# Projections of q, k and v as three float32r products of split operands

## The reference

```
xn  = (x - mean) / sqrt(var + 1e-5)                 # over the 256 features
kqv = xn @ Wqkv + bqkv                              # 256 -> 768
q, k, v = kqv as (b, s, 3, 16 heads, 16)
scores = einsum('bsnh,btnh->bnst', k, q) / 4
scores = triu(scores) - 10000 * tril(ones, -1)
attn = softmax(scores, axis=2)
out  = einsum('bnkq,bknh->bqnh', attn, v) @ Wo + bo
ffn  = fp8(xn / in_scale) * in_scale @ (w8 * w8_scale).T
result = x + out + ffn
```

## Time and profile before

| | |
|---|---|
| time, median of 3 runs | 254.98 us (254.64 to 255.24) |
| span of the profiled execution | 251.8 us; its time around the span is not listed apart |
| TensorE busy (products) | 188.6 us, 75% |
| VectorE busy | 181.1 us, 72% |
| GpSimd busy | 101.3 us, 40% |
| ScalarE busy | 96.5 us, 38% |
| mean granted TensorE clock | 0.897 of 2.4 GHz |
| chain of waits, by engine | TensorE 41%, VectorE 20%, SyncE's queue 16%, issue 8%, DMA 8%, GpSimd 4%, ScalarE 2% |

### The profile page before, as it was taken

One profiled execution on the slowest core, in us unless ns is written; L12 is line 12 of the kernel. 1 busy time (PEld: TensorE's weight loads), 2 busy tenths in 40 slices (PEclk: granted clock), 3 DMA queues, 4 the chain that ended last, 5 costly groups with the idle time before them and its releaser, 6 DMA issues.

```text
span 251.8 us, 5223 instructions
## 1 busy us (share of the span) xinstructions
PE 188.6 (75%) x1725; PEld 140.4 (56%) x1725; DVE 181.1 (72%) x371; ACT 96.5 (38%) x167; POOL 101.3 (40%) x127
## 2 busy tenths in 40 slices
PE   5685026103949898899699969996999698789893
PEld 5564024003736576578477847783878375555572
DVE  3999108501999797987979797978497958995342
ACT  3242200000434464355345623752356135435530
POOL 6605000000488429524842564274425642622410
PEclk9799557555699999999999999997799889999999
DMA  5941696084024734661546273346052725001002
GB/s 187 281 140 38 182 270 167 20 189 110 2 85 120 189 87 127 148 179 46 164 107 171 76 204 95 116 124 178 18 161 80 198 51 157 4 0 46 3 3 83
DMA packets 30102, 28.99 MB, mean 115 GB/s; under 512 B 3008, under 2 KB 26500, under 8 KB 30084
## 3 DMA queue, kind: packets, MB, share of 16 engines
q1 hardware_dynamic: 30084, 28.75, 42.2%
HBM read 17.11 MB, written 10.75 MB: 111 GB/s over the span
## 4 chain that ended last, share of the span: by engine, by line
PE 41%; DVE 20%; SPq 16%; issue 8%; DMA 8%; POOL 4%; ACT 2%; DVEq 1%; POOLq 0%; ACTq 0%
SPq L322 10%; PE pso L984 6%; DVE row_max L732 6%; DMA k_stack<-k_scratch 5%; PE bankA L1072 4%; PE bankA L1009 4%; PE bankB L1009 4%; PE ps L960 3%; PE ps L937 3%; SPq L379 3%; SPq L368 3%; DMA q_scratch<-q_parts 3%; PE ps L939 2%; PE ps L965 2%; DVE neg_parts L750 2%
## 5 line engine op out<-in xcount | busy, mean ns | idle before, releaser
L479 POOL TENSOR_SCALAR_AFFINE_SELECT probs<-probs 128x512 f32<-128x512 f32 (+1 forms) x48 | 38.0, 792 | 122.4 <-ACT probs L541 122.4
L732 DVE TENSOR_REDUCE row_max<-ps 128x4 f32<-128x1024 f32 (+1 forms) x48 | 58.2, 1216 | 28.3 <-PE ps L932 25.1
L541 ACT ACTIVATE probs<-ps 128x1024 f32<-128x1024 f32 x48 | 49.0, 1024 | 72.0 <-PE ps L960 67.7
L932 PE MATMUL ps<-k_stack,q_stack 125*128 125x128 bf16 x128 | 10.6, 230 | 33.1 <-DMA k_stack<-k_scratch 29.9
L932 PEld LDWEIGHTS ps<-k_stack,q_stack 125*128 125x128 bf16 x128 | 8.8, 102 | 35.1 <-issue 30.6
L937 PE MATMUL ps<-k_stack,q_stack 96*128 96x128 bf16 x128 | 20.3, 236 | 5.1 <-DVE row_max L732 5.1
L984 PE MATMUL pso<-probs,v_sb 128*32 128x256 f32 x256 | 21.8, 414 | 0.1
L960 PE MATMUL ps<-q_stack,k_stack 99*128 99x256 bf16 x128 | 20.8, 290 | 0.5 <-issue 0.5
L939 PE MATMUL ps<-k_stack,q_stack 125*128 125x128 bf16 x128 | 20.2, 234 | 0.0
L1009 PE MATMUL bankB<-xT,wqk_sb 128*128 128x256 f32 x64 | 17.7, 423 | 1.4 <-ACT xT L589 1.4
L937 PEld LDWEIGHTS ps<-k_stack,q_stack 96*128 96x128 bf16 x128 | 13.2, 106 | 8.6 <-DVE row_max L732 8.1
(11 more groups left out here) (129 smaller groups left out, 387.8 us busy)
## 6 DMA issues: line engine op xcount, KB each, us to landing
k_stack<-k_scratch SPq DMA_DIRECT2D x32, 192.0 KB, 4.0
q_scratch<-q_parts SPq DMA_DIRECT2D x32, 128.0 KB, 2.0
k_scratch<-k_parts SPq DMA_DIRECT2D x32, 128.0 KB, 1.9
q_stack<-q_scratch SPq DMA_DIRECT2D x16, 256.0 KB, 4.0
q_stack<-q_scratch SPq DMA_DIRECT2D x16, 192.0 KB, 3.0
out_dram<-y SPq DMA_DIRECT2D x8, 256.0 KB, 3.0
x_all<-in_L_attn_x_dram SPq DMA_DIRECT2D x1, 1536.0 KB, 9.0
x_all<-in_L_attn_x_dram SPq DMA_DIRECT2D x2, 256.0 KB, 3.1
```

The lines of the kernel that those rows point to most:

```text
L479: pool.affine_select(out=v, in_=v, compare_op=ALU.is_ge, fill=0.0, base=0, pattern=[[0, heads], [1, P]], channel_multiplier=-1).then_inc(c ...
L541: act.activation(probs[:, i % 2, :], ps[:], ACT.Exp, scale=SCALE).then_inc(exp_done, 1)
L732: dve.tensor_reduce(dst, src, AX_X, ALU.max).then_inc(max_done, 1)
L932: mm = pe.matmul(ps[:, h * P:h * P + P], q_stack[0:K_MAX, par, hh, 0:P], k_stack[0:K_MAX, par, hh, 0:P], start=True, stop=True)
```

## The change

Each of xT and the weights gets a high part, rounded to float32r by a copy, and a low part, the difference. A projection is then low weights by high x, high weights by low x, and high by high, all in float32r, added up in PSUM: 12 matmuls where there were 4 float32 products. The low part of x is made by VectorE, which waits for ScalarE's second copy (xT itself, which `clip_x` still reads), so that the two engines don't read bank B together.

```diff
@@ ScalarE, xT_out @@
+                act.activation(xT_hi[:, par], bank["B"][:].rearrange("p (k s) -> p k s", k=KT), ACT.Copy).then_inc(xT_hi_ready, 1)
                 act.activation(xT[:, par], bank["B"][:].rearrange("p (k s) -> p k s", k=KT), ACT.Copy).then_inc(xT_ready, 1)
@@ ScalarE, startup @@
-                ins = act.activation(wqk_sb[:, k].rearrange("p (m d h) -> p m d h", m=2 * KT, d=HD),
+                ins = act.activation(wqk_hi[:, k].rearrange("p (m d h) -> p m d h", m=2 * KT, d=HD),
...
+            act.wait_ge(wv_landed, 2 * 16)
+            act.activation(wv_hi[:], wqkv_sb[:, :, 2 * D:], ACT.Copy).then_inc(wv_hi_ready, 1)
@@ VectorE @@
+            def xT_low(b, par):
+
+                dve.wait_ge(xT_ready, b + 1)
+                wait(dve, v_mm, b - 1)
+                dve.tensor_tensor(xT_lo[:, par], bank["B"][:].rearrange("p (k s) -> p k s", k=KT),
+                                  xT_hi[:, par].bitcast(F32), ALU.subtract).then_inc(xT_lo_ready, 1)
+
+            def weights_low():
+
+                dve.wait_ge(w_ordered, 1)
+                for k in range(KT):
+                    ins = dve.tensor_tensor(wqk_lo[:, k].rearrange("p (m d h) -> p m d h", m=2 * KT, d=HD),
+                                            wqkv_sb[:, k, 0:2 * D].rearrange("p (m h d) -> p m d h", m=2 * KT, d=HD),
+                                            wqk_hi[:, k].bitcast(F32).rearrange("p (m d h) -> p m d h", m=2 * KT, d=HD), ALU.subtract)
+                ins.then_inc(wqk_lo_ready, 1)
@@ VectorE, run: behind negate_and_split(n, 1), ahead of maxima(n + 1, 1) @@
+                if st.does("xT"):
+                    xT_low(n + 2, p)
@@ VectorE, startup @@
+                    weights_low()
+                    xT_low(0, 0)
...
             rest1(0, 0, "k", "A")
+            xT_low(1, 1)
...
             rest1(1, 1, "k", "A")
+            dve.wait_ge(wv_hi_ready, 1)
+            dve.tensor_tensor(wv_lo[:], wqkv_sb[:, :, 2 * D:], wv_hi[:].bitcast(F32), ALU.subtract).then_inc(wv_lo_ready, 1)
@@ TensorE, project_qk @@
-                pe.wait_ge(xT_ready, b + 1)
+                pe.wait_ge(xT_hi_ready, b + 1)
+                pe.wait_ge(xT_lo_ready, b + 1)
...
                     for k in range(KT):
-                        mm = pe.matmul(dst[:, m * S:m * S + S], wqk_sb[:, k, col:col + P], xT[:, par, k, :],
-                                       start=(k == 0), stop=(k == KT - 1))
+                        pe.matmul(dst[:, m * S:m * S + S], wqk_lo[:, k, col:col + P], xT_hi[:, par, k, :],
+                                  start=(k == 0), stop=False)
+                        pe.matmul(dst[:, m * S:m * S + S], wqk_hi[:, k, col:col + P], xT_lo[:, par, k, :],
+                                  start=False, stop=False)
+                    for k in range(KT):
+                        mm = pe.matmul(dst[:, m * S:m * S + S], wqk_hi[:, k, col:col + P], xT_hi[:, par, k, :],
+                                       start=False, stop=(k == KT - 1))
```

More of the change, by code:

```diff
@@ L33 @@
 F32 = mybir.dt.float32
+F32R = mybir.dt.float32r
 I32 = mybir.dt.int32
@@ L169, in build @@
         wqkv_sb = sb("wqkv_sb", [P, KT, 3 * D])
-        wqk_sb = sb("wqk_sb", [P, KT, 2 * D])
+        wqk_hi = sb("wqk_hi", [P, KT, 2 * D], F32R)
+        wqk_lo = sb("wqk_lo", [P, KT, 2 * D], F32R)
+        wv_hi = sb("wv_hi", [P, KT, D], F32R)
+        wv_lo = sb("wv_lo", [P, KT, D], F32R)
         wo_sb = sb("wo_sb", [P, KT, D])
@@ L207, in build @@
         xT = sb("xT", [P, 2, KT, S])
+        xT_hi = sb("xT_hi", [P, 2, KT, S], F32R)
+        xT_lo = sb("xT_lo", [P, 2, KT, S], F32R)
         x_over = sb("x_over", [P, KT, S])
@@ L266, in build @@
         xn_ready, xT_mm, xT_ready = sem("xn_ready"), sem("xT_mm"), sem("xT_ready")
+        xT_hi_ready, xT_lo_ready = sem("xT_hi_ready"), sem("xT_lo_ready")
+        wqk_lo_ready, wv_hi_ready, wv_lo_ready = sem("wqk_lo_ready"), sem("wv_hi_ready"), sem("wv_lo_ready")
         q_mm, k_mm, v_mm = sem("q_mm"), sem("k_mm"), sem("v_mm")
@@ L284, in build @@
         out_landed = [sem(f"out_landed{p}") for p in range(2)]
-        read = {"xT": (xT_ready, 1, 1), "q": (rest_ready, 2, 1), "k": (rest_ready, 2, 2),
+        read = {"xT": (xT_lo_ready, 1, 1), "q": (rest_ready, 2, 1), "k": (rest_ready, 2, 2),
                 "v": (v_ready, 1, 1), "max_h0": (max_rows_ready, 2, 1), "max_h1": (max_rows_ready, 2, 2),
@@ L1003, in project_qk @@
                 j = "qk".index(qk)
-                pe.wait_ge(xT_ready, b + 1)
+                pe.wait_ge(xT_hi_ready, b + 1)
+                pe.wait_ge(xT_lo_ready, b + 1)
                 dst = take(st, bk, qk)
                 for m in range(KT):
+                    col = j * D + m * P
                     for k in range(KT):
-                        col = j * D + m * P
-                        mm = pe.matmul(dst[:, m * S:m * S + S], wqk_sb[:, k, col:col + P], xT[:, par, k, :],
-                                       start=(k == 0), stop=(k == KT - 1))
+                        pe.matmul(dst[:, m * S:m * S + S], wqk_lo[:, k, col:col + P], xT_hi[:, par, k, :],
[5 more added lines that the diff above has]
+                                       start=False, stop=(k == KT - 1))
                 mm.then_inc((q_mm, k_mm)[j], 1)
@@ L1021, in project_v @@
             def project_v(st, b, par):
-                pe.wait_ge(xT_ready, b + 1)
-                tokens_by(take(st, "B", "v"), xT[:, par], wqkv_sb[:, :, 2 * D:]).then_inc(v_mm, 1)
+                pe.wait_ge(xT_lo_ready, b + 1)
+                dst = take(st, "B", "v")
+                for t in range(TB):
+                    tok = slice(t * P, t * P + P)
+                    for k in range(KT):
+                        pe.matmul(dst[:, t * D:t * D + D], xT_lo[:, par, k, tok], wv_hi[:, k, :],
+                                  start=(k == 0), stop=False)
+                        pe.matmul(dst[:, t * D:t * D + D], xT_hi[:, par, k, tok], wv_lo[:, k, :],
+                                  start=False, stop=False)
+                    for k in range(KT):
+                        mm = pe.matmul(dst[:, t * D:t * D + D], xT_hi[:, par, k, tok], wv_hi[:, k, :],
+                                       start=False, stop=(k == KT - 1))
+                mm.then_inc(v_mm, 1)
             def transpose_max(st, b, half, bk):
@@ L1100, in _ @@
             pe.wait_ge(w_ordered, 1)
+            pe.wait_ge(wqk_lo_ready, 1)
             for b in range(2):
@@ L1106, in _ @@
             pe.wait_ge(wv_landed, 2 * 16)
+            pe.wait_ge(wv_hi_ready, 1)
+            pe.wait_ge(wv_lo_ready, 1)
             project_v(None, 0, 0)
```

## The result

| | before | changed |
|---|---|---|
| median of 18 runs each | 256.49 us | 255.72 us |
| lowest and highest | 254.64 to 261.03 | 251.15 to 258.38 |
| ratio of the runs compared | | 0.9858 (95%: 0.9822 to 0.9893) |
| span and own time of the profiled execution | 251.8 us, not known | 252.3 us, 254.03 |
| mean granted clock | 0.897 | 0.876 |

The medians lie 0.3% apart, the ratio says 1.4%. It is taken over the runs within 1.5% of each kernel's fastest, and the changed kernel's times lie in two groups, 9 of 251.15 to 254.51 and 9 of 256.93 to 258.38, of which only the lower one counts, while 17 of the 18 runs of the kernel before do. The forecast was 1.1 us slower; why the times of one kernel lie so far apart is the main question of what follows.

What follows compares the result with a forecast made beforehand. Bound by SyncE's queue at startup, the k projection and VectorE's chain in steps, then clock falls. Span 251.8 plus 5 x 0.2 and 0.1 for step 0 gave 252.9; plus 3.2, 256.1 us, range 252.6 to 262.

Steps and rivals of the forecast that it cites:

- the delay of q: In each full step, TensorE starts the projection of q 0.90 us later, waiting for the low part of x.
- the shift of phase 1 of slot 2: In a full step, the q projection before this phase ends 0.49 us later.
- v off the path: The projection of v gets 0.41 us shorter, ahead of a product that waits for o_sum: nothing gained.
- the idle time ahead of ffn: TensorE's idle time before the ffn product grows from 1.8 to about 2.3 us in every step.
- the price of the falls: Two falls of the clock in steps 3 to 5 cost 4.57 us in all, about 2.3 us a fall.
- B: Rival: the clock falls in more steps, one to three more falls, 258.4 to 263 us, taken as 259.5; chance 0.27.
- D: Rival: the clock falls in fewer steps, 251.5 with both falls gone, 253.8 with one, taken as 253; chance 0.23.
- the way from the span to the median: The median was put 3.2 us above the span of the profiled execution, 254.98 against 251.8 us.
- step 0 at nothing gained: In step 0, the low part of x goes into time otherwise spent stretched: 0, at most 0.9 us; 0.1 summed.
- The size of the schedule's cost: Each of 5 steps gets 0.2 us longer, 1.0 us in all; bounds 0 to 0.5 a step.
- the other 0.12 of the forecast, from GpSimd's queue: The split of k on GpSimd starts late and stretches VectorE's operations: 0.2 us a step rather than 0.08.
- The startup: Added work before the steps, below 9 us, is covered by 11 us of idle time behind SyncE's issues: 0.

Runs made afterwards that it cites:

- the fourth trace: The changed kernel, not edited further, traced a fourth time: span 250.2 us, no fall of the clock in steps 1 to 5.

## Why the prediction was wrong

**Right:** the cost of a product (0.11 forecast, 0.12 measured), the delay of q (0.90; 0.88), the shift of phase 1 of slot 2 (0.49; 0.55), the beat at full clock (+0.2; 23.8 against 23.55), v off the path, the idle time ahead of ffn (2.3; 2.13).

**Wrong, the clock as one price for the kernel.** This is the step of the prediction that failed: the price of the falls, taken over from one trace. The forecast was 1.1 us slower; the ratio says 1.4% faster, the medians 0.3% faster, and two later comparisons 1.1% and 0.3% slower. The working kept the two falls of the one trace, 4.57 us, as a constant in the span, and took B and D as cases of which one would come true. Both come true, from execution to execution: 0 falls in steps 1 to 5 in one trace of the changed kernel, 5 in two. The term varies between 0 and about 11 us: steps 1 to 5 add up to 119.4 us without a fall and to 130.4 with five. Of the traced executions 251.9 us had no fall in steps 1 to 5, 254.0 had three and the quick step 0, 257.8 had four and the quick step 0, 263.4 and 264.0 had five and one more in step 6. So the lower group of times, which the ratio counts, is not simply D: an execution with three falls lies in it. B's mechanism fits too, 3.4 falls on average over five traces against 2.0 over three of the kernel before, but so few traces don't show it. The 0.5 us that the forecast called measurable is far below the spread of either kernel. Even in the one trace the price was a little off: one fall was in step 4, which takes 23.93 us at full clock and not 23.57, so the two cost 4.3 us.

**Wrong, the way from the span to the median.** The working added 254.98 - 251.8 = 3.2 us around the span. All later runs have 1.7 to 1.9. The profiled execution of before thus took about 253.7 us; its median over 18 runs is 256.49. With 1.7 the sum would have been 254.6 us for an execution with two falls. That 256.1 stands beside a measured 255.72 is luck: none of the 18 runs of the changed kernel lies between 254.51 and 256.93.

**Wrong, step 0 at nothing gained.** The working had the low part of x go into time that would be spent stretched, and stopped there. It missed that exponential 2, and so GpSimd's causal 2, can come late enough for x_big to slip in ahead of it: about 1.2 us less in step 0, in two of five traces, both times where the clock had fallen during the wait for the low part. A fall is a cost in steps 1 to 5 and went with a gain here, so no single price per fall holds.

**The size of the schedule's cost.** A usual step is 0.25 us longer, as said, but the sum behind it came out by luck. The two projections gave back 0.33 and 0.30 us where 0.41 each was forecast, so phase 1 of slot 3 moved by 0.26 and not by 0.08 (10.13 against 9.87); the other 0.12 of the forecast, from GpSimd's queue, did not appear, since k_rest and ffn moved by 0.26 and 0.27. Most runs of steps 1 to 5 also have an odd step (23.25 in the changed kernel, 23.93 in the one before), and with it the five sum to the same 118.9; the fourth trace has no odd step and 119.41. Forecast +1.0 us, measured 0.0 to 0.5.

**The startup.** The first phase 1 stood at 35.88 us against 36.11, as forecast. Over all traces of the two kernels, with and without idle products, it came at 35.0 to 36.1 before the change and at 35.6 to 36.2 after it, and step 0 began at 59.79 us on average against 60.42: the startup that was put at 0 costs about 0.6 us.

What stays open: what decides, in an execution, whether the clock falls behind an idle time of 2 us, and so why the first 18 times fall into two groups; and what the upper half of the times of the kernel before is made of. The falls can be taken away, and that was tried; they could not be called at will.

## What to carry to other kernels

When a product gets faster but its end isn't waited for, the time saved turns into idle time of TensorE, and a fall of the clock behind it costs more than was saved: ask what the granted clock does there. Where the times of one kernel spread over several us, take several traces before pricing anything from one, and compare steps at equal clock, or hold the clock with products that nobody reads, before giving a difference to an edit. When operands are split in two, use the part that is ready first in the first products, and free the PSUM bank before the second part is made. The cheaper products gave back 0.6 us a step and no more than the longer way of x cost; these edits together, which were not tried apart, took another 0.4 (23.8 to 23.37) and brought the step below the 23.55 of before.

## What the runs showed of the hardware

- A float32r product with 128x256 moving columns is one record, 0.12 us from start to start, against 2 x 0.216 for float32 and 0.11 for bfloat16.
- The clock fell to 1.2 GHz around or behind idle times of TensorE of 1.6 to 2.2 us, in some executions and not in others. 12 to 16 bfloat16 products in that gap kept it at 2.4 GHz in steps 1 to 5 in all six filled traces.
- A VectorE operation of 0.43 us took 1.19 when GpSimd's had begun first, and a 128x16 one of 0.16 took 1.12; which of two operations 0.1 to 0.4 us apart started first went with a step of 23.9 or 25.1 us.
